# A gather queue that rests by a count of small writes instead of by a wait for its own last transfer

## The reference

```python
q = (x @ Wq + bq).reshape(n, H, C)
k = (x @ Wk + bk).reshape(n, H, C)
v = (x @ Wv + bv).reshape(n, H, C)
attn = jnp.einsum('nhc,mhc->hnm', q, k) / np.float32(np.sqrt(C))
mask = adj == 0.0
...
e = jnp.where(mask[None], 0.0, jnp.exp(neg - jnp.where(all_inf, 0.0, m)))
alpha = e / jnp.where(denom == 0.0, 1.0, denom)
out = jnp.einsum('hnm,mhc->hnc', alpha, v)
...
beta = jax.nn.sigmoid(jnp.concatenate([out, x_r, out - x_r], axis=-1) @ Wb)
return beta * x_r + (1.0 - beta) * out
```

## Time and profile before

| | |
|---|---|
| time, median of 3 runs (lowest, highest) | 1977.79 us (1976.16, 1981.87) |
| the profiled execution's own time | 1964.78 us |
| its span, first to last instruction | 1962.9 us |
| busy: DVE, POOL, PE, ACT | 1310.3, 1174.4, 1164.9, 839.9 us |
| POOL's transfers | 1023 gathers, 62 scatters, 63 stores |
| mean of one gather on POOL | 1001 ns |
| moved by DMA | 438.70 MB, 223 GB/s over the span |

### The profile page before, as it was taken

The page is one execution under the profiler, slowest core; times in us unless marked ns, Lnnn a source line. Parts: engine busy times, 40 slices in busy tenths (PEclk is TensorE's granted clock), DMA queues, the critical chain, the costliest instruction groups (busy, mean ns, idle before and its releaser), DMA issues.

```text
span 1962.9 us, 20126 instructions
## 1 busy us (share of the span) xinstructions
PE 1164.9 (59%) x4696; PEld 680.4 (35%) x4696; DVE 1310.3 (67%) x3389; ACT 839.9 (43%) x1595; POOL 1174.4 (60%) x1711
## 2 busy tenths in 40 slices
PE   7322746657574756466655657756766668444553
PEld 5101433334342334233323334423423334233342
DVE  5876878666756776557656468757555677886564
ACT  2331443334643463344634348545635476431112
POOL 4454565566566656656566656565665665676664
PEclk9565677677776776667777578876667767666565
DMA  9947856666755776564866668776767778433331
GB/s 334 354 164 199 318 198 233 214 233 223 293 197 183 258 271 234 216 218 161 342 230 215 247 243 294 265 258 247 252 217 278 249 255 280 140 89 96 94 89 57
DMA packets 130037, 438.70 MB, mean 223 GB/s; under 512 B 26567, under 2 KB 61198, under 8 KB 97150
## 3 DMA queue, kind: packets, MB, share of 16 engines
q1 hardware_dynamic: 76510, 297.15, 41.1%
q0 software_dynamic: 52832, 136.07, 22.5%
q10 hardware_dynamic: 576, 4.19, 0.5%
HBM read 417.93 MB, written 19.44 MB: 223 GB/s over the span
## 4 chain that ended last, share of the span: by engine, by line
POOL 34%; issue 24%; DVE 13%; DMA 13%; PE 7%; DVEq 4%; another core or an unknown queue 3%; ACT 2%; SPq 1%; ACTq 0%; POOLq 0%
POOL s_kv L799 31%; DMA s_kv<-kv_rows,s_rec_in 11%; DVE s_raw L1248 2%; DVE s_kv L1246 2%; PE s_acc L1001 1%; DVEq L1296 1%; DVE s_wtop L1295 1%; POOL node_records L766 1%; POOL out_rows L775 1%; ACT s_mask L1023 1%; DVEq L1443 1%; DVE s_kv L1272 1%; DVE s_d_max L1454 1%; PE s_ps_key L889 1%
## 5 line engine op out<-in xcount | busy, mean ns | idle before, releaser
L799 POOL DMA_INDIRECT s_kv<-kv_rows,s_rec_in x1023 | 1024.3, 1001 | 700.6 <-DMA s_kv<-kv_rows,s_rec_in 340.6
L829 PE MATMUL s_ps_w<-s_mask,s_bit_w 128*128 128x512 bf16 x1008 | 374.6, 521 | 332.4 <-ACT s_mask L1023 233.8
L1023 ACT ACTIVATE s_mask<-s_adj_in 128x2048 bf16<-128x2048 f32 x252 | 478.2, 1900 | 114.5 <-DMA s_adj_in<-in_adj 66.7
L1001 PE MATMUL s_acc<-s_kv,ident 128*128 128x128 f32 x2032 | 321.3, 330 | 109.9 <-DVE s_kv L1272 62.8
L1001 PEld LDWEIGHTS s_acc<-s_kv,ident 128*128 128x128 f32 x2032 | 312.2, 244 | 137.4 <-DVE s_kv L1272 77.3
L829 PEld LDWEIGHTS s_ps_w<-s_mask,s_bit_w 128*128 128x128 bf16 x1008 | 111.3, 120 | 559.1 <-ACT s_mask L1023 294.9
L1246 DVE TENSOR_TENSOR s_kv<-s_kv,s_ps_q 128x1536 f32<-128x1536 f32 (+15 forms) x76 | 147.1, 1935 | 235.2 <-DMA s_kv<-kv_rows,s_rec_in 224.3
L1272 DVE TENSOR_TENSOR s_kv<-s_kv,s_ps_q 128x1536 f32<-128x1536 f32 (+15 forms) x76 | 146.7, 1931 | 17.9 <-ACT s_ps_q L1062 10.1
L1062 ACT ACTIVATE s_ps_q<-s_sc 128x56 f32<-128x56 f32 (+17 forms) x76 | 16.7, 220 | 318.4 <-DVE s_sc L1262 218.5
L1248 DVE TENSOR_REDUCE s_raw<-s_kv 128x48 f32<-128x1536 f32 (+15 forms) x76 | 147.1, 1935 | 5.6
L1050 ACT COPY s_xs<-s_ps_x 128x128 f32<-128x128 f32 x63 | 16.6, 264 | 288.7 <-remote 160.4
(11 more groups left out here) (281 smaller groups left out, 1563.2 us busy)
## 6 DMA issues: line engine op xcount, KB each, us to landing
s_adj_in<-in_adj SPq DMA_DIRECT2D x248, 1024.0 KB
s_kv<-kv_rows,s_rec_in POOLq DMA_INDIRECT x1023
kv_rows<-s_kv SPq DMA_DIRECT2D x16, 512.0 KB, 7.6
s_rec_in<-node_records SPq DMA_DIRECT2D x55, 106.0 KB
s_kv<-in_x_cols SPq DMA_DIRECT2D x4, 1024.0 KB, 8.4
s_adj_in<-in_adj ACTq DMA_DIRECT2D x4, 1024.0 KB
s_d_in<-in_x_cols SPq DMA_DIRECT2D x8, 512.0 KB
s_d_v<-kv_rows SPq DMA_DIRECT2D x8, 512.0 KB
```

The costliest lines, as they stand in the source:

```text
L799: nc.gpsimd.indirect_dma_start(out=kv[0:n, START[k] + s], out_offset=None, in_=kv_dram[:, :], in_offset=bass.IndirectOffsetOnAxis(ap=rec_i ...
L829: last = nc.tensor.matmul(w[:], bit_w[:, slab], mask[:, k % 2, s * WORD:(s + 1) * WORD], start=False, stop=(slab == SLABS - 1))
L1001: last = nc.tensor.matmul(acc[:, c * D:(c + 1) * D], ident[:], kv[:, START[k] + s, D:2 * D], start=(s == 0), stop=(s == plain(k) - 1))
L1023: nc.scalar.activation(mask[:, q % 2], adj_in[:, q % ADJ_RING], ACT.Sign, accum_out=edges[:, t, h:h + 1]).then_inc(masked, 1)
```

## The change

Where the last gather belongs to a unit below 63, a pause is no longer a wait. POOL writes zeros over the whole of `l_o` eight times, and after each write executes a DRAIN. From unit 63 on the pause is the old wait.

```diff
 RUN = 12
+REST = 8
...
             def pause_after(n):
                 if begun["since"] + n > RUN and begun["last"] is not None:
                     k, s = begun["last"]
-                    pool.wait_ge(gathered[k % FLIGHT], slots_landed(k) - 16 * (HELD[k] - 1 - s))
+                    if k < OVER_AT:
+                        for _ in range(REST):
+                            nc.gpsimd.memset(l_o[:], 0.0)
+                            pool.drain()
+                    else:
+                        pool.wait_ge(gathered[k % FLIGHT], slots_landed(k) - 16 * (HELD[k] - 1 - s))
                     begun["since"] = 0
                 begun["since"] += n
```

## The result

The changed kernel takes 2211.42 us, the median of 4 runs (2208.22 to 2217.14); the kernel before took 1976.97 in the same runs (1967.95 to 1981.87). The ratio is 1.1195, with a 95% interval of 1.1147 to 1.1243: 12% slower. The forecast was 2691 us, 36% slower. The direction and the engine were right, the size was wrong by a factor of three, and the time lies in the stated range only because that range reached into the second rival's case.

A forecast was written before the change was run, and what follows sets the result against it. POOL was taken as the bound, by transfer starts and 85 pauses. A pause of 3.53 + 7.25 + 1.75 = 12.53 us instead of 4.19 added 709 us to 1962.9: span 2672, median 2691 us, range 2090 to 2950.

The forecast's parts named there:

- second rival: In a pause, the DRAIN waits for the landing and no longer: 2128 us, or 2217 with 0.40 a write; chance 0.22.
- POOL as the bound, and a pause's excess reaching the end: On POOL, 1015 starts of about 1.3 us and 85 pauses set the span; a pause's gain or loss reaches the end.
- everything else has cover: Beside POOL, DVE, ACT, PE and SP's loads have slack or follow the units; nothing gets faster to pay anything back.
- Removed, 85 pauses of 4.19 us over the 0.30: On POOL, the change removes 85 waits of 4.19 us over the usual 0.30 idle: 356 us.
- The landing, 3.53 us: In each pause, the landing of gathers still counts: 1.75 us as when quiet plus 1.78 of shrunken excess, 3.53 us.
- The DRAIN past the landing, 7.25 us: In each pause, the first DRAIN behind up to twelve transfers outlasts their landing by 7.25 us.
- as at the end: Upper bound for a pause's first DRAIN, from the program's closing DRAIN of 9850 ns: landing plus 7.25 us.
- the number of transfers ahead: Rival: a DRAIN's price rises with the transfers ahead, twelve here against five at the end; beyond 2950 us, chance 0.06.
- the way to the next transfer: On POOL, from a pause's end to the next transfer: the usual 0.30 us of idle.
- The seven writes, 0.25 us each: In each pause, the seven drained writes after the first cost 0.25 us each, 1.75 in all (1.4 to 2.8).
- The cheap DRAIN: First rival: a pause is only eight drained writes, 2.0 us instead of 4.19; median 1847 us (1790 to 1870), chance 0.13.
- The run isn't broken by writes: Rival: without the landing, later POOL transfers slow down; with a cheap DRAIN it could eat 186 us; no change, 0.02.

The follow-up runs named there:

- e1: The changed kernel with its DRAINs gone, POOL waiting for each of the eight writes by a semaphore that the write increments: 1820.46 us, ratio 0.9335.
- e9: The kernel before with a DRAIN behind each of its last six stores: one run of 1969.07 us, before 1970.06.
- e4: The kernel before with three times (DRAIN, small write) behind its last store: one run of 1955.59 us, before 1953.43.
- e10: The changed kernel with six writes a pause, each waited for by its own semaphore, and no DRAIN: 1775.28 us, ratio 0.9012.
- e13: The changed kernel with five semaphore-waited writes a pause and no DRAIN: 2014.73 us in the fastest run, 2045.75 to 2052.24 in the others.
- e12: The kernel before with 16 DRAINs, each behind a pause's wait, 12 to 162 transfers since the last one: one run of 2006.95 us, before 1971.63.
- e6: The kernel before with (small write, DRAIN) twice behind its last store: one run of 1962.42 us, before 1961.93.
- e2: The changed kernel with the loop of writes and DRAINs replaced by `pass`, so no pause there: 2110.35 us, ratio 1.0822.

## Why the prediction was right in direction and wrong in size

**POOL as the bound, and a pause's excess reaching the end: right.** 247.6 us more idle on POOL, 244.6 more span. No other engine gave anything back, as "everything else has cover" said.

**Removed, 85 pauses of 4.19 us over the 0.30: right.** Between the transfers' ends and starts they measure 4.42 us, which is 4.12 over it. (The pause that ends at 1750.81 is the first of the old waits that stay; the last of the 85 ends at 1732.73.)

**The landing, 3.53 us: right in kind, nearly so in size.** 3.44 us of a pause is landing, and with no DRAIN (e1) it is gone.

**The DRAIN past the landing, 7.25 us: this step failed.** It measured 1.02. I saw one instance of a POOL DRAIN behind transfers, asked only what kind of instruction stood ahead of it ("a software transfer just issued"), and took its price as the price of that kind. The price goes by the number of indirect transfers since the last DRAIN. At the end of the program before, that number is all 1148, beyond the point where the price stays at 9.8 us. In a pause it is mostly twelve, and 0.04 + 12 x 0.082 = 1.02 is what the pause shows. (With one transfer the formula gives 0.12, while e9's short DRAINs end 0.43 us past the landing; below twelve it isn't measured with the landing over.) The closing's own excess was read a little low: the DMA records put its last landing at 1954.92, not 1955.4, so it outlasted the landing by 7.73 us. The bound "as at the end" was therefore true as a bound and useless as a value. The 6.23 us too many, times 85, are 530 us. The writes (0.42 a pause too few) and the way to the next transfer (0.79 where I had 0.30) take back 77, the landing adds 8: 460 of the 464.5 us by which the forecast's span of 2672 exceeds the 2207.5. The trace held the hint: the long DRAIN stood in a stretch in which nothing moved, so it was doing something of its own, and I never asked what could have piled up for it. One of my own rivals named "the number of transfers ahead", but counted since the last pause, five at the end against twelve; counted since the last DRAIN it would have turned the sign and given the answer.

**The seven writes, 0.25 us each: within its bounds (0.20 to 0.40), a little low.** 0.32 measured from start to start, 2.17 us for the seven and not 1.75. The closest case was the second rival at its dear end, a DRAIN up to the landing and 0.40 a write: 2217 us against 2211.42. It met the sum by luck: its 2.8 us of writes stood for 2.17 and its wait was kept at the old length, and both together made up for the 1.02 past the landing that it left out.

**The cheap DRAIN: false of a DRAIN, true of a pause.** Its 2.3 us pause exists (e1: 2.44) once the writes wait on a semaphore of their own; it promised 1847 us and e1 gave 1820.46. The Trainium skill (VectorE: DVE Perf Modes, section "The DRAIN you can't avoid"), which the prediction names, has about 12 ns for the DRAINs of a program's beginning and end. POOL's measured 0.17 us even with nothing accumulated (e4), 1.02 behind twelve transfers and 9.8 behind 1148.

**"The run isn't broken by writes": refuted.** Writes break it if the pause that they make lasts 1.80 us (e10), and don't at 1.54 (e13).

What stays open: what it is that a long run of POOL's transfers uses up so that other engines' starts are held, and why 1.54 us of pause after twelve transfers isn't enough while 1.80 is. The rows show the holding up and the length; nothing in them names the resource, and the part of the recording is untested. That the DRAIN's price and this effect have one cause is possible; no run here tests it.

## What to carry to other kernels

An instruction seen once has a price under one history: before it is multiplied by 680, ask what has accumulated since the last of its kind, and put that number beside the one it will have in its new place. To let an engine rest, wait for something that the engine finishes itself; a DRAIN or a gather's semaphore makes it wait for the memory as well. And find the rest's length from both sides, since here one write too few cost 239 us or more and two too many 45.

## What the runs showed of the hardware

- A DRAIN of POOL waits for the landing of its indirect transfers (the change against e1). With them landed it costs 0.04 us and 0.082 for each since the last DRAIN, up to 96; from 141 on it stays near 9.8 us (e12). It ends 0.42 to 0.45 us past the landing of a single store (e9); with none since, it takes 0.16 to 0.17 (e4), 0.04 and 0.05 for the closing's in e6 and e9.
- A write of 128x128 f32 on POOL is 0.21 us; 0.26 from start to start when the engine waits for it by a semaphore (e1), 0.32 by a DRAIN (the change).
- Indirect transfers 1.3 us apart on POOL, without a pause, hold up starts on PE and DVE, as far as these traces can say: 2110.35 us without pauses, 1775.28 with 85 of 1.9 us (e2, e10). With four, five, six, eight and twelve semaphore-waited writes a pause: 2043, 2015 to 2052, 1775, 1820 and 1889 us.
